# Expert stage of a mixture-of-experts block: 39 unrolled tiles of 256 rows in place of a loop over 72 blocks of 128

## What is computed

```
logits = x2 @ router_w                      # x2: 4096 tokens x 256, 8 experts
top_p, top_e = top_k(softmax(logits), 2)    # two experts for each token
for each of the 8192 (token, expert) rows:
    h = gelu(row @ w_in[e] + b_in[e])       # 256 -> 256
    y = (h @ w_out[e] + b_out[e]) * p
out = sum of both y of a token              # times tanh(gate), added to the residual
```

## Time and profile before

| | us |
|---|---|
| median of 3 runs | 632.7 (628.24 to 634.42) |
| span of the profiled execution, first to last instruction | 627.0 |
| what lies around that span, against the median | 5.7 |
| pair stage, until the last scatter of rows | 0 to 410 |
| from there to the first transposition of the expert stage | 410 to 420.2 |
| expert stage | 420.2 to 585.3 |
| last stage | 585.3 to 627.0 |

### The profile page before, as it was taken

The page is one execution under the profiler, slowest core; times in us unless marked ns, Lnnn a source line. Parts: engine busy times, 40 slices in busy tenths (PEclk is TensorE's granted clock), DMA queues, the critical chain, the costliest instruction groups (busy, mean ns, idle before and its releaser), DMA issues.

```text
span 627.0 us, 16108 instructions
## 1 busy us (share of the span) xinstructions
PE 428.4 (68%) x4440; PEld 317.7 (51%) x4441; DVE 393.6 (63%) x1594; ACT 330.8 (53%) x763; POOL 237.5 (38%) x283
## 2 busy tenths in 40 slices
PE   1146787778777887788778667118979969899200
PEld 0124555556555665566556544016757757677100
DVE  4357667786778677867696541665545535555397
ACT  1223657765676567655766555106646636566100
POOL 7122232355345544554344222413434424434200
PEclk9978899999999999999999896559999979999755
DMA  7603455455544564446435551167434324311498
GB/s 204 143 1 94 143 169 152 141 170 163 161 127 118 149 171 136 111 135 180 142 104 144 169 159 45 51 143 195 128 103 129 120 81 133 113 53 69 169 362 315
DMA packets 75931, 87.67 MB, mean 140 GB/s; under 512 B 10109, under 2 KB 66922, under 8 KB 75754
## 3 DMA queue, kind: packets, MB, share of 16 engines
q1 hardware_dynamic: 69354, 69.21, 38.5%
q0 software_dynamic: 6528, 17.87, 7.6%
HBM read 54.49 MB, written 32.55 MB: 139 GB/s over the span
## 4 chain that ended last, share of the span: by engine, by line
PE 33%; ACT 18%; issue 16%; DVE 15%; DMA 8%; SPq 4%; POOL 3%; ACTq 2%; DVEq 1%; POOLq 0%
PE ps_J L935 7%; PE ps_G L935 5%; PE ps_O L1093 4%; PE ps_F L935 3%; ACT prob L801 3%; DMA y_got<-store_y 3%; ACT xn_E L788 3%; PE ps_T L961 3%; PE ps_S L935 3%; PE ps_O L989 3%; ACT h_f L909 2%; PE ps_S L980 2%; ACT h_hi L914 2%; DVE y_out L1614 2%; ACT xn_C L788 1%
## 5 line engine op out<-in xcount | busy, mean ns | idle before, releaser
L755 POOL DMA_INDIRECT store_y<-y_out,y_row x72 | 69.2, 961 | 108.3 <-DVE y_out L1614 105.6
L801 ACT ACTIVATE prob<-ps_S 128x512 f32<-128x512 f32 x128 | 69.2, 596 | 27.5 <-PE ps_S L980 27.5
L720 POOL DMA_INDIRECT store_x<-xn_E,slot_u x64 | 63.2, 987 | 28.6 <-issue 16.5
L1604 DVE TENSOR_TENSOR h_lo<-h_f,h_hi 128x256 f16<-128x256 f32 x72 | 30.6, 425 | 65.9 <-ACT h_hi L914 57.9
L980 PE MATMUL ps_S<-q_stack,k_stack 128*128 128x256 f16 x256 | 40.2, 281 | 18.5 <-ACT prob L801 12.0
L989 PE MATMUL ps_O<-prob,v_wide 128*32 128x128 f32 x1024 | 42.6, 286 | 0.0
L1496 DVE SCALAR_TENSOR_TENSOR xs<-ps_O,tanh_g,xs 128x512 f32 (+1 forms) x16 | 12.0, 751 | 47.8 <-PE ps_O L1093 47.8
L741 POOL TENSOR_TENSOR x<-moved,x_in 128x256 f32<-128x256 f32 x32 | 22.5, 725 | 43.1 <-DVE moved L1448 43.1
L1093 PE MATMUL ps_O<-wo_t,av 128*128 128x256 f32 x128 | 33.6, 408 | 5.2 <-ACT av L856 5.2
L980 PEld LDWEIGHTS ps_S<-q_stack,k_stack 128*128 128x128 f16 x256 | 22.8, 99 | 25.8 <-ACT prob L801 16.1
L909 ACT ACTIVATE h_f<-ps_J,bin_t 128x128 f32<-128x128 f32 x72 | 22.6, 364 | 23.1 <-PE ps_J L935 22.7
(11 more groups left out here) (240 smaller groups left out, 1519.6 us busy)
## 6 DMA issues: line engine op xcount, KB each, us to landing
xb<-store_x SPq DMA_DIRECT2D x72, 128.5 KB, 2.2
parts_scratch<-parts SPq DMA_DIRECT2D x32, 256.0 KB, 2.2
k_stack<-parts_scratch SPq DMA_DIRECT2D x64, 128.0 KB
q_stack<-parts_scratch SPq DMA_DIRECT2D x128, 64.0 KB
y_got<-store_y SPq DMA_DIRECT2D x16, 512.0 KB, 5.6
x_in<-in_x SPq DMA_DIRECT2D x16, 256.0 KB, 2.9
c_in<-in_ctx SPq DMA_DIRECT2D x16, 256.0 KB, 3.1
c_again<-in_ctx SPq DMA_DIRECT2D x16, 256.0 KB, 4.6
```

Of the source, the lines that this page charges most:

```text
L720: pool.indirect_dma_start(store_x, bass.IndirectOffsetOnAxis(slot_u[q][:, at:at + 1], 0), xn_e[q][:, at, :], None).then_inc(s_scat[q], 16)
L755: pool.indirect_dma_start(store_y, bass.IndirectOffsetOnAxis(y_row[i.n % FAR][:, :], 0), y_out[i.n % FAR][:, :], None).then_inc(s_y_kept[i ...
L801: ins = act.activation(prob[m % PROBS][:, 2 * n:2 * n + 2, :, :], bank_s[n], ACT.Sigmoid, scale=float(HD) ** -0.5)
L1604: dve.tensor_tensor(h_lo[q][:, :, :], h_f32[q][:, :, :], h_hi[q][:, :, :], ALU.subtract)\
```

## The change

The expert stage has 39 tiles of 256 rows (`BLK`, `SUB` = 2 halves of 128). All are written out, there is no loop, and registers are read from `table` eight at a time (`CHUNK`), two tiles ahead of use. The steps of the engines keep their order. There are 5 buffers of 256 rows for `xb` (`XB`) and for `y_out` and `y_row` (`YB`). The first layer's products have 256 moving columns, the second layer's 12 products 256 columns (6 for each half), and POOL issues two indirect DMAs for a tile.

The padding is zeroed from the addresses in `running` after the last pair but one: 512 rows for each expert (`PAD`), which takes in every place where the last pair can put a row (up to 256) and 256 beyond. DVE makes `pad_rows` at the end of body 19, and POOL waits for the padding before the four scatters of the last pair, which then write over it. The spare tiles, seven of 256 rows, are zeroed by SP after body 5 and no longer at the start.

```diff
-CAP = TOKENS + 128
-FAR = 18
-BLOCKS = -(-((TOP * TOKENS + NE * 127) // 128) // FAR) * FAR
+BLK = 256
+SUB = BLK // 128
+CAP = TOKENS + BLK
+TILES = (TOP * TOKENS + NE * (BLK - 1)) // BLK
+XB, YB, CHUNK = 5, 5, 8
...
-            for i in range(SPARES):
-                sp.dma_start(store_x[NE * CAP + 128 * i:NE * CAP + 128 * i + 128, :], zeros[:, :])\
-                    .then_inc(s_spare, 16)
             for t in range(LOOP_FROM):
                 matrices(t)
                 body(Step(t), {s for s, lag in LAG.items() if 0 <= t - lag < NP})
+            zero_rows = zeros[:, :].unsqueeze(1).broadcast_to([128, SUB, WIDE])
+            for i in range(SPARES):
+                sp.dma_start(store_x[NE * CAP + BLK * i:NE * CAP + BLK * i + BLK, :]
+                             .rearrange("(b p) c -> p b c", b=SUB), zero_rows).then_inc(s_spare, 16)
...
-            sp.wait_ge(s_plan, PAD_STEPS)
+            sp.wait_ge(s_pad_at, 1)
...
-                sp.dma_start(store_x[bass.ds(at, 128), :], zeros[:, :]).then_inc(s_pad, 16)
+                sp.dma_start(store_x[bass.ds(at, PAD), :].rearrange("(b p) c -> p b c", b=PAD // 128),
+                             zeros[:, :].unsqueeze(1).broadcast_to([128, PAD // 128, WIDE])).then_inc(s_pad, 16)
...
-                    scatter(t - LAG["F"])
+                    f = t - LAG["F"]
+                    if f.reg is None and f.n == NP - 1:
+                        pool.wait_ge(s_pad, 16 * NE)
+                    scatter(f)
...
+            for i in range(TILES):
+                n = i % YB
+                pool.wait_ge(s_y_out, i + 1)
+                for b in range(SUB):
+                    pool.indirect_dma_start(store_y, bass.IndirectOffsetOnAxis(y_row[n][:, b:b + 1], 0),
+                                            y_out[n][:, b, :], None).then_inc(s_y_kept[n], 16)
...
+            for i in range(-2, TILES):
+                if i + 2 < TILES:
                     transpose_block(i + 2)
+                if 0 <= i + 1 < TILES:
+                    layer1(i + 1)
+                if i >= 0:
+                    layer2(i)
...
+            def beside(t):
+                matrices(t)
+                if t - LAG["F"] == NP - 2:
+                    dve.wait_ge(s_r, RANK_STEPS * (NP - 1))
+                    dve.tensor_copy(pad_rows[:, :], running[0:1, :]).then_inc(s_pad_at, 1)
+
+            run_bodies(dve, body, after_first=setup, beside=beside)
```

More of the change, by code:

```diff
@@ L165, in run_bodies @@
             beside(t)
[L168 to L203, removed]
 def build(nc, x, ctx, mask, gates_in, temp, bp, sim, wall, wp, wu, wo, w_in, b_in, w_out, b_out, decay, eye, before,
@@ L474, in build @@
         s_spare = sem("spare_rows_zeroed")
-        s_xb = [sem(f"block_loaded{i}") for i in range(FAR)]
+        s_pad_at = sem("padding_rows_known")
+        s_xb = [sem(f"block_loaded{i}") for i in range(XB)]
         s_xb_t = sem("block_transposed")
@@ L485, in build @@
         s_y_out = sem("expert_output_made")
[L486 removed]
+        s_y_kept = [sem(f"expert_output_scattered{i}") for i in range(YB)]
         s_got = [sem(f"outputs_loaded{i}") for i in range(PICK_BUFS)]
@@ L497, in build, with plan_reader, load, entry @@
                    for i in range(2)]
-        store_x = nc.dram_tensor("store_x", (NE * CAP + SPARES * 128, WIDE), F32, kind="Internal").ap()
+        store_x = nc.dram_tensor("store_x", (NE * CAP + SPARES * BLK, WIDE), F32, kind="Internal").ap()
         store_y = nc.dram_tensor("store_y", (LEFT + TOP * TOKENS, D), F32, kind="Internal").ap()
         block = st.enter_context(nc.Block())
[L504 to L515, removed]
-                             else table[0:1, row_at, bass.ds(at, n)])
-                return [bass.RuntimeValue.of_register_unchecked(x).with_bounds(min_val=0, max_val=top) for x in regs]
-            return entries
+        def plan_reader(eng, line, top):
+            row_at, known = LINES.index(line), {}
+            def load(c):
+                regs = [eng.alloc_register(f"{line}_{c + k}") for k in range(CHUNK)]
+                eng.reg_load(regs, table[0:1, row_at, c:c + CHUNK])
+                for k, x in enumerate(regs):
+                    known[c + k] = bass.RuntimeValue.of_register_unchecked(x).with_bounds(min_val=0, max_val=top)
+            def entry(i, ahead=2):
+                for j in (i, i + ahead):
+                    if j < PLANNED and j not in known:
+                        load(j // CHUNK * CHUNK)
+                return known[i]
+            return entry
         @block.sync
@@ L910, in gelu @@
                                    bias=biases[:, bass.ds(at + m, 1)]).then_inc(s_gelu, 1)
[L911 to L913 removed]
+                act.wait_ge(s_gelu, KT * (i + 1))
+                if i >= 2:
+                    act.wait_ge(s_y, i - 1)
                 act.activation(h_hi[q][:, :, :], h_f32[q][:, :, :], ACT.Copy).then_inc(s_h_hi, 1)
[L916 to L917 removed]
+            for i in range(-2, TILES - 1):
+                if i + 2 < TILES:
                     copy_hi(i + 2)
[L919 to L923 removed]
+                if i + 1 >= 0:
+                    gelu(i + 1)
         @block.tensor
```

214 lines of the change are left out of this document (98 added, 116 removed).

## The result

The changed kernel takes 610.6 us (median of 5 runs, 608.6 to 616.0) against 631.0 us (5 runs, 628.2 to 634.4) for the kernel before: ratio 0.9685, 95% interval 0.9638 to 0.9733. On record stood 629 us with a range of 613 to 641. The execution that was profiled is the slowest of the five, 616.0 us with a span of 614.2. Some executions are in a slower state, whatever the kernel: ratios and intervals leave these out, medians do not.

The account below looks back on a forecast made before the run. PE, with the way through ACT and DVE, was taken to bound the expert stage. Stage -31.5, padding +23.2, read and load +0.1, spares -1.1 and +4.0, end +1.3 sum to -4.0: 629 us, range 613 to 641.

Parts of the forecast that it names:

- the stage: Expert stage: larger tiles and short register reads bring it from 165.1 to 133.6 us, -31.5 us (-23 to -36).
- I take 160: Padding: 4.21 MB of zero rows flow at 160 GB/s for 26.3 us, making the path +23.2 us longer.
- Rival A: Zero rows flow at full rate, 341 GB/s: padding +9.2, spares 0, total 611 us; chance 0.15.
- The two times that I had named: Signs at the padding: last zero row landing at 435 us, PE's first transposition near 446.
- 4 x 1.5 = 6 us: Expert stage: four register reads of 8 entries idle PE for 1.5 us each, 6 us (3 to 15).
- PE has nothing queued behind the read: Expert stage: the reason given why each register read's time counts in full on PE.
- Rival C: Expert tiles: step set by scatters or the ACT and DVE way, not PE; 0.5 us longer each, 647 us; chance 0.07.
- I take +4: Spares after body 5: seven DMAs, 1.85 MB, delay the next pair's stacks and `c_in`; +4 us (0 to +7.5).
- -1.1: Start: without spares ahead of the second pair's loads, `sim_inv` moves up by 1.1 us, its other input made at 22.26.
- The term of +1.3: End of the expert stage: the last tile's two scatters run one behind the other, +1.3 us.
- Rival B: Zero rows flow at 131 GB/s as at the start: padding +29.0, spares +7.5, total 638 us; chance 0.15.
- its rate term: Within the forecast of 620 to 637 us (chance 0.60), the zero-row rate alone reaches 5 us down.

Follow-up runs that it names:

- late_idle_b: Changed kernel with spares zeroed after body 1 and 256 padding rows per expert zeroed after the last pair's ranks, repeated with more rounds: 643.24 us, ratio 0.9661.
- sq_after: The changed kernel repeated unedited in a later session, on a chip like the first: 610.5 us, ratio 0.9663 against the kernel before.
- the square: Four kernels on one chip: spares after body 5 or 1, padding early (512 rows) or late (256); 610.5 us unedited, 607.6 spares, 600.9 padding, 596.5 both.
- after_again: The changed kernel once more, unedited, on one of the three slower chips: 651.5 us, ratio 0.9894 against the kernel before.
- the deeper pipeline: Spares after body 1 and late 256-row padding, plus transposing tile i + 4 and first layer of i + 2 beside second layer of i: 651.78 us, ratio 0.9836.

## Why the prediction was wrong, step by step

The large terms had the right sign. The sum was 15.0 us too high (-4.0 against -19.0): 11.1 from the padding and 6.6 from the stage, of which the spares and the last stage take 2.8 back.

**Padding, "I take 160".** This is the step that failed most. The term came out as +12.2 us in place of +23.3. Eight DMAs of 512 rows flowed from 415.1 to 432.5 us, 4.21 MB in 17.4 us, 242 GB/s in place of 160; by the prediction's own sum 26.3 - 17.4 = 8.9 us. I read a price for each byte from windows in which each DMA wrote adjacent rows, and carried it to rows 128 apart. The adjacent mapping has 171 to 212 GB/s in the experiment and costs 4.6 us more on the path (36.4 against 31.8 us), so the mapping explains about half of the 8.9 us. The rest is that 160 was low for adjacent rows as well; it came from windows of 1 or 2 us, of DMAs with 128 rows, partly beside scatters, and which of these made it low is not shown. Rival A named the mapping but gave it 341 GB/s, which no window of a sustained flow reached (317 from 416 to 418 us, then 238 to 247). Its time, 611 us, is the measured one by luck: +9.2 for padding and 0 for spares where the runs have +12.2 and +4.6, made up for by the stage.

The other 2 us are smaller terms. Completion took 1.0 us (432.5 to 433.5) and not 1.9. From there to SP's read are 6.7 us and not 7.5, since I counted one scatter twice: the last scatter of the kernel before starts at 586.53, not at 585.26, and its 2.37 us to landing begin with that start. The two times that I had named, 435 for the last zero row and 446 for the first transposition, nearly came in the first profile (433.5 and 443.9), but by luck: its last logits were 11.2 us late and not 2.9.

**Register reads, "4 x 1.5 = 6 us".** Nothing: PE is busy for 40.00 of 40 us across them. Two things were wrong. The read of 8 takes 0.60 to 0.77 us on PE, as in the row with 0.74 us, from which I had moved away to the long ones of 19; that is half of the term. And "PE has nothing queued behind the read" does not hold: the products go on without a gap. The run with 18 entries shows that the length goes with the number read at once. By the row the term would have been 4 x 0.74 = 3.0 us; without it the stage is 127.6 + 1.3 us, a change of -36.2 against -36.8 measured. The sentence on the page "Runtime: NRT & Kernel Launch" of the Trainium skill ("Instruction fetch mechanics") has some 200 ns a register for loads from HBM. Reads from a tile in this case don't follow it: 8 entries take 0.52 to 0.86 us, 18 take 1.4 to 4.7. An estimate from the page's figure would be 1.6 and 3.6 us.

**Tiles.** Right: 3.06 us for a step (3.12 predicted), 0.109 us for a product, PE full, the others with a third of their time free. Rival C, that the step is not PE's, is refuted on this chip. On the three slower ones the step is some 3.5 us (stages of 145.5 to 152.9 us), but in `late_idle_b` it is not by the scatters that the rival named: DVE's row numbers, which would wait for them, are not among the waits there.

**Spares, "I take +4" and "-1.1".** The gain at the start was 0.2 us, not 1.1: `kv` of pair 1 came 4.6 us earlier (17.67 in place of 22.31), but `sim_inv` began at 23.20 in place of 23.39, and `kv` of pair 2 at 43.8 in place of 44.1. I had taken the other input of `sim_inv` as fixed, and it moved: `sim_sq` was made 0.86 us later (22.97 in place of 22.11). The timelines show where that comes from. The changed kernel, with its `kv` at 17.67:

```profile
17.73 1.00 DVE L1188 SCALAR_TENSOR_TENSOR shift_B<-mv_B,rstd_B 128x2 f32<-128x2 f32 x1 [0.82 <-POOL rstd_B L670]
```

And the kernel with the spares at the start, with its `kv` at 25.86:

```profile
17.73 0.16 DVE L1188 SCALAR_TENSOR_TENSOR shift_B<-mv_B,rstd_B 128x2 f32<-128x2 f32 x1 [0.82 <-POOL rstd_B L670]
```

Beside POOL's `kv`, DVE's small operation took 1.00 us in place of 0.16, and all behind it on DVE, ACT and PE came later by that. After body 5 the step is 6.2 us longer, by the mechanism named (the stacks and `c_in` behind the packets), and 4.5 us in `sq_after`; by the square 2.9 to 4.4 us of it reach the end. The sum of +2.9 compares with +4.6 in the profile.

**The end and the last stage.** The term of +1.3 for the last tile's second scatter is part of the -36.8 and can't be told from it: POOL's last scatter starts 3.1 us behind the start of the last `y_out` (570.21 to 573.32), where before it was 0.7 us (585.82 to 586.53). Rival B, zero rows at 131 GB/s, is refuted.

**The range** was too narrow at its lower end, since its rate term went down by 5 us only and the reads were not allowed to vanish: at 242 GB/s and no reads my sum is -4.0 - 8.9 - 6 = -18.9, 613.8 us, at the very edge of the range.

## What to carry to other kernels

A rate read from a DMA of one shape holds for that shape: ask where the rows lie, not only how full the engines are. Zeroing ahead of a scatter puts the scatter behind the zeros, and is paid with its bytes wherever nothing else runs; issue background writes where queue and engines are idle, and as late a padding as possible with as few rows as a block needs. Read registers in small batches, close to use, since large ones can cost far more than in proportion. An operation that a change moves forward on one engine can slow another engine's beside it: look at what will run at the new time.

## What the runs showed of the hardware

**Chips differ by 5%, in places and not throughout.** On three of the four numbered chips the pairs of the loop come 23 us apart in place of 20.6, with bodies 0 to 5 within some 3 us of their usual times. The list of waits of `after_again` (us in total, times, longest) has rows that are not there in the changed kernel on the first chip (`remote` is the profile's name for a release that it ties to none of the engines listed):

```profile
ACT ct_hi L749 <- remote: 35.9, 8, 5.2
...
ACT xb_hi L869 <- remote: 9.8, 6, 2.1
```

In `late_idle_b` on such a chip `ct_hi` waits so in each of the ten pairs of the loop, for 4.5 to 4.8 us in eight of them, against 1.8 to 2.2 in `sq_after` (timelines of ACT, the second line from `sq_after`):

```profile
228.82 0.60 ACT L748 ACTIVATE ct_hi<-ps_T 128x512 f16<-128x512 f32 x1 [4.60 <-remote]
...
220.09 0.60 ACT L749 ACTIVATE ct_hi<-ps_T 128x512 f16<-128x512 f32 x1 [2.17 <-PE ps_T L929]
```

The difference of some 2.5 us is that of the pairs' periods. The expert stage of `late_idle_b` (timeline of PE, ACT and DVE):

```profile
508.14 0.60 PE L1086 MATMUL ps_R<-ident,xb 128*128 128x128 f32 x4
...
510.96 0.60 ACT L868 ACTIVATE xb_hi<-ps_R 128x512 f16<-128x512 f32 x1 [2.18 <-remote]
...
511.07 0.69 DVE L1584 TENSOR_TENSOR y_out<-ps_S,bout_t 128x512 f32<-128x512 f32 x1 [1.56 <-remote]
```

PE's products for `ps_S` and `ps_R` end by 508.7, but ACT and DVE both begin on them only at 511.0, nearly together, and so in every second tile (every 7.0 us from 475.9 to 525.1). PE goes on with products of other tiles meanwhile, runs dry later, and a pair of tiles takes 7.0 us (503.97 to 510.96 in this timeline) in place of 6.11. In the deeper pipeline such a wait is up to 3.1 to 4.0 us and nothing is won. So it looks as if signals of PE arrived late while it ran a long unbroken row of products; this is a reading, not shown. The other candidate is the fetching of code. The Trainium skill ("Runtime: NRT & Kernel Launch", "Instruction fetch mechanics") says that a taken branch can force a fetch that holds up the engine. This alone does not fit: `ct_hi` waits in every pair, though a round of the loop with its one branch has two, and the tiles are unrolled. The cause is open and was not tried further. It matters for the change: it gains 3.2% and 3.4% on the two good chips and 1.1% on one of the others, where no run had a full PE stage.
